# A mixture-of-experts kernel on Trainium2: TensorE's expert numbers loaded once for six tiles instead of once for each

## What is computed

```python
logits = xt @ Wr + br
probs = jax.nn.softmax(logits, axis=-1)
top_p, top_idx = jax.lax.top_k(probs, 2)
weights = top_p / top_p.sum(axis=-1, keepdims=True)
xn = (xt - mu) * jax.lax.rsqrt(var + LN_EPS)
xe = xn[None, :, :] * ln_g[:, None, :] + ln_b[:, None, :]
h = jax.nn.gelu(jnp.einsum('end,edh->enh', xe, W1) + b1[:, None, :], approximate=False)
y = jnp.einsum('enh,ehd->end', h, W2) + b2[:, None, :]
sel = jnp.take_along_axis(jnp.transpose(y, (1, 0, 2)), top_idx[:, :, None], axis=1)
out = (weights[:, :, None] * sel).sum(axis=1)
```

## Time and profile before

| | |
|---|---|
| median of 3 runs | 1020.41 us (1019.91 to 1022.8) |
| the profiled execution's own time | 1021.31 us |
| its span in the profile | 1019.3 us |
| PE busy | 752.5 us, 74% |
| PEld busy | 647.6 us, 64% |
| DVE busy | 611.3 us, 60% |
| ACT busy | 583.5 us, 57% |
| POOL busy | 483.2 us, 47% |

### The profile page before, as it was taken

How to read it: one execution, slowest core, us unless ns; L and a number is a source line. 1 busy time by engine, 2 the same in 40 slices (tenths; PEclk the granted TensorE clock), 3 DMA queues, 4 the chain that set the end, 5 groups by cost and what they waited for, 6 DMA issues and landing times. The chain is left out here.

```text
span 1019.3 us, 24538 instructions
## 1 busy us (share of the span) xinstructions
PE 752.5 (74%) x7306; PEld 647.6 (64%) x7307; DVE 611.3 (60%) x1820; ACT 583.5 (57%) x1157; POOL 483.2 (47%) x539
## 2 busy tenths in 40 slices
PE   2787795655579555542199999999959899899995
PEld 1665695444469544420178878888748788788784
DVE  6556402633752467977077877787736666666663
ACT  2667734655553435341176767767637677667763
POOL 4566400000275720577445656665545555555554
PEclk9989998567689879757599999999989999999998
DMA  7978413644311484412533333333323333333340
GB/s 222 235 231 258 116 32 106 183 125 143 115 56 37 156 251 142 139 56 75 182 98 114 111 119 113 118 117 109 111 85 90 112 106 113 114 116 110 110 123 29
DMA packets 127285, 126.87 MB, mean 124 GB/s; under 512 B 22471, under 2 KB 95454, under 8 KB 127106
## 3 DMA queue, kind: packets, MB, share of 16 engines
q1 hardware_dynamic: 92914, 82.73, 27.9%
q0 software_dynamic: 15296, 34.64, 9.6%
q10 hardware_dynamic: 19024, 8.86, 3.1%
HBM read 79.48 MB, written 49.09 MB: 126 GB/s over the span
## 5 line engine op out<-in xcount | busy, mean ns | idle before, releaser
L967 DVE TENSOR_TENSOR AB<-AB 128x512 f16<-128x512 f32 x280 | 192.3, 687 | 73.9 <-ACT AB L603 68.6
L397 POOL DMA_INDIRECT row_dram<-rows,idx x128 | 127.2, 994 | 203.3 <-DVE rows L775 165.3
L425 POOL DMA_INDIRECT row_dram<-B x140 | 144.0, 1029 | 111.8 <-DVE B L973 77.2
L425 POOL DMA_INDIRECT out<-B x140 | 140.1, 1001 | 116.4 <-DVE B L973 91.1
L600 ACT ACTIVATE AB<-ps 128x512 f16<-128x512 f32 x280 | 168.1, 600 | 41.3 <-PE ps L1155 40.4
L1172 PE MATMUL ps<-PPb,AB 128*128 x1120 | 185.3, 219 | 0.0
L1173 PE MATMUL ps<-PPb,AB 128*128 x1120 | 185.2, 219 | 0.0
L603 ACT ACTIVATE AB<-ps 128x512 f32<-128x512 f32 x280 | 169.1, 604 | 0.0
L1153 PE MATMUL ps<-B,PPb 128*128 128x256 f16 x560 | 154.7, 276 | 0.5 <-issue 0.5
L1154 PE MATMUL ps<-B,PPb 128*128 128x256 f16 x560 | 154.3, 276 | 0.0
L1155 PE MATMUL ps<-B,PPb 128*128 128x256 f16 x560 | 154.3, 275 | 0.0
(11 more groups left out here) (201 smaller groups left out, 1483.7 us busy)
## 6 DMA issues: line engine op xcount, KB each, us to landing
B<-row_dram SPq DMA_DIRECT2D x70, 264.0 KB
B<-row_dram SPq DMA_DIRECT2D x70, 136.0 KB
rows<-in_x SPq DMA_DIRECT2D x32, 256.0 KB, 5.0
rows<-in_L_conv_protein_pair SPq DMA_DIRECT2D x16, 512.0 KB, 4.3
g_dram<-work ACTq DMA_DIRECT2D x32, 256.0 KB, 3.1
work<-g_dram SPq DMA_DIRECT2D x32, 256.0 KB, 2.7
ABT<-in_x SPq DMA_DIRECT2D x32, 256.0 KB, 3.0
ABT<-in_L_conv_protein_pair SPq DMA_DIRECT2D x16, 512.0 KB, 4.0
```

What stands on the lines that cost most here:

```text
L397: pool.indirect_dma_start(row_dram, bass.IndirectOffsetOnAxis(ap=idx[:, j:j + 1], axis=0), rows[:, j, :], None).then_inc(scattered[b], 16)
L425: pool.indirect_dma_start(out_rows if second else row2_dram, bass.IndirectOffsetOnAxis(ap=Rw[:, u, b, at:at + 1].bitcast(u32), axis=0), Rw ...
L967: dve.tensor_tensor(Hp[:, hs, 1, :], Hf[:, q, :], Hp[:, hs, 0, :], ALU.subtract).then_inc(h_parts[q], 1)
```

## The change

The table `experts` becomes one number for each step, with zeros in front and behind. TensorE has seven registers, and one load fills all seven with the experts of seven tiles in a row, enough for six steps, as a step needs those of two neighbouring tiles. The load stands in the last of the six steps (`u == RING - 1`), between the first and the second half of the up products; `begin` copies the two that a step needs (`nc.snap`) at the step's head, and loads by itself only at the beginning of each list. The two waits at L1128 and L1148 are left out. `two_lists` passes the step's place in the ring to `before`, and a stage named in `always` also runs in steps whose tile lies outside the list.

```diff
--- before.py
+++ after.py
@@ -60,16 +60,16 @@
             extra()
 
 
-def two_lists(eng, stages, depth, before=None):
+def two_lists(eng, stages, depth, before=None, always=None):
 
     longest = max(lag for lag, _ in stages)
     for second, low, high in ((0, 0, CUT), (1, CUT, TILES)):
 
         def step(n, u):
             if before:
-                before(n)
+                before(n, u, low)
             for lag, stage in stages:
-                if not isinstance(n, int) or low <= n - lag < high:
+                if not isinstance(n, int) or low <= n - lag < high or stage is always and n + 1 < high + longest:
                     stage(n - lag, (u - lag) % RING, second)
 
         def single(n0, n1):
@@ -175,8 +175,8 @@
         first_row = work[0:1, 1024:1024 + TILES].bitcast(i32)
 
         EFRONT = 3
-        EROWS = TILES + EFRONT
-        experts = work[0:1, 1408:1408 + 2 * EROWS].bitcast(i32).rearrange("p (n v) -> p n v", v=2)
+        EROWS = TILES + EFRONT + RING
+        experts = work[0:1, 1408:1408 + EROWS].bitcast(i32)
 
         class Choice:
 
@@ -909,8 +909,7 @@
             step(dve.tensor_tensor(Q[:, 0:NQ], Q[:, 0:NQ], passed, ALU.add))
             step(dve.tensor_scalar(Q[:, 0:NQ], Q[:, 0:NQ], float(NE * CT), None, ALU.min))
             dve.sem_inc(s.Q_done, 1)
-            dve.memset(experts[:, 0:EFRONT, :], 0)
-            dve.memset(experts[:, TILES:, :], 0).then_inc(s.fill_done, 1)
+            dve.memset(experts, 0).then_inc(s.fill_done, 1)
             fs = [0]
 
             def fstep(i):
@@ -943,9 +942,9 @@
             assert fs[0] == FSTEPS, fs
             dve.wait_ge(s.tbl_psum, 1)
             dve.wait_ge(s.fill_done, 1)
-            for v, table in enumerate((first_row, experts[:, EFRONT:, 0], experts[:, EFRONT - 1:EFRONT - 1 + TILES, 1])):
+            for v, table in enumerate((first_row, experts[:, EFRONT:EFRONT + TILES])):
                 i = dve.tensor_copy(table.rearrange("p (l t) -> p l t", l=LISTS),
-                                    ps[6 + min(v, 1)][0:1, 0:LISTS * P].rearrange("p (l t) -> p l t", l=LISTS)[:, :, 0:CUT])
+                                    ps[6 + v][0:1, 0:LISTS * P].rearrange("p (l t) -> p l t", l=LISTS)[:, :, 0:CUT])
             i.then_inc(s.tbl_done, 1)
 
             def norm(n, u, second):
@@ -1124,28 +1123,27 @@
                     pe.wait_ge(r_loaded[u], (n // RING) * 16 + 16)
                 else:
                     pe.wait_ge(s.xn_done, n + 1)
-                if not isinstance(n, int) or n >= 2:
-                    pe.wait_ge(s.xT_lo, n - 1)
                 for b in range(HALVES):
                     i = pe.transpose(ps[u % 2][:, b * P:(b + 1) * P], Rw[:, u, b, ROW:ROW2], ident[:, :])
                 i.then_inc(s.xT_psum, 1)
 
+            PEQ = [mybir.EngineType.PE]
+            coming = [pe.alloc_register(f"expert{k}") for k in range(RING + 1)]
             chosen = []
 
             def load_experts(n):
-
-                _, chosen[:] = nc.values_load_multi_w_load_instructions(
-                    experts[:, bass.ds(n, 1), :].rearrange("p n v -> p (n v)"), [mybir.EngineType.PE],
-                    min_val=0, max_val=NE - 1,
-                    skip_runtime_bounds_check_because="each is an expert of the table, or the zero beside them")
+                pe.reg_load(coming, experts[:, bass.ds(n, RING + 1)])
+
+            def begin(n, u, low):
+                if isinstance(n, int) and n == low:
+                    load_experts(n - u)
+                chosen[:] = [nc.snap(r, PEQ, min_val=0, max_val=NE - 1) for r in coming[u:u + 2]]
 
             def up(n, u, q):
 
                 hs = 2 * (u % 2) + q
                 x_ = chosen[1]
                 pe.wait_ge(s.xT_lo, n + 1)
-                if not isinstance(n, int) or n >= 2:
-                    pe.wait_ge(h_full[q], n - 1)
                 for k in range(2):
                     c = (2 * q + k) * P
                     w = lambda r: W1h[:, bass.ds(x_, 1), r, c:c + P].rearrange("p a m -> p (a m)")
@@ -1176,8 +1174,12 @@
                         if k == HC - 1:
                             i.then_inc(y_psum[b], 1)
 
-            two_lists(pe, [(1, xT), (2, lambda n, u, second: up(n, u, 0)), (2, lambda n, u, second: up(n, u, 1)),
-                           (3, lambda n, u, second: down(n, u))], 2, before=load_experts)
+            def next_experts(n, u, second):
+                if u == RING - 1:
+                    load_experts(n + 1)
+
+            two_lists(pe, [(1, xT), (2, lambda n, u, second: up(n, u, 0)), (0, next_experts), (2, lambda n, u, second: up(n, u, 1)),
+                           (3, lambda n, u, second: down(n, u))], 2, before=begin, always=next_experts)
 
 
 def kernel(**inputs):
```

## The result

| | median, us | runs |
|---|---|---|
| before, run beside it | 1021.61 (1019.91 to 1026.94) | 4 |
| after | 1011.64 (1010.24 to 1015.59) | 4 |

The ratio is 0.990, with a 95% interval of 0.985 to 0.995: faster by 1.0%, where 2.7% was predicted (993, range 976 to 1009). The direction is right and the size is not. The profiled execution took 1011.25 us with a span of 1008.9, so its steps can be laid beside those of before (1021.3 and 1019.3).

A forecast was written before the change was run, and what follows sets the result against it. TensorE's instruction stream was taken to bound the second list, a three-step transfer loop also to limit the first. Gains of 20 and 7 us gave -27 from 1021.3: 994, or 993 as a median; range 976 to 1009.

The forecast's parts named there:

- What bounds before, and how long an ordinary step can be: Second list: bound by TensorE's instruction stream at 3.50 us a step; the array alone would allow 3.02.
- The waits: TensorE's three dropped waits, already satisfied when reached: 0.3 to 0.4 us of sequencer work in all; they "end nothing".
- The sequencer's lead: TensorE's sequencer would be 0.4 us ahead of the array where the new load stands, mid up products.
- The load of seven: New load once in six steps: 1.0 us, stalling the array 0.65 us per six steps.
- Rival A: The load of seven is dear, 1.9 us: second list 3.33 a step, first about 3.42, total 1005; chance 0.2.
- The branch: Loop branch every sixth step on TensorE: some 0.25 us of stall, the sequencer having regained only 0.3 after the load.
- transfer loop: Second list: mix, store, load, landing and products over four steps, 12.1 us or 3.03 a step, under the forecast 3.17.
- scatter: Second list: transfer loop near the step's 3.17 us, so scatter costs a little, making 3.20.
- For the first list the loop: Three-step loop of mix, store, load and norm, 9.94 to 10.30 us: 3.37 a step for 3.48, gaining 7 us.
- GpSimd's issue: First list's loop: second store's issue takes 1.34 us, 0.98 undisturbed; the 0.36 is part of the 10.30 us turn.
- rival C: Transfers bind both lists as stores land later: second list 3.35, gain 10, first gains 2, total 1008; chance 0.1.

The follow-up runs named there:

- waits_ring8: Kernel before with the three waits left out, two numbers still loaded each step, and a ring of eight slots: 988.88 us, 0.967 of before.
- before_ring8: Kernel before with a ring of eight slots instead of six, tiles moved to the scattered rows' memory: 1014.03 us, 0.990 of before.
- quads6: Kernel after, six slots, padded table, two loads of four numbers (fourth and sixth step) instead of one of seven: 1002.60 us, 0.978 of before.
- after_ring8: Kernel after with a ring of eight slots and one load of nine numbers per eight steps: 967.82 us, 0.947 of before.
- aligned6: Kernel after, six slots, table padded so each load of seven starts on a 16-byte boundary: 1008.64 us, 0.984 of before.
- load_ring8: Kernel before, waits kept, with a ring of eight slots and one load of nine numbers per eight steps: 972.19 us, 0.953 of before.

## Why the prediction was off

**What bounds before, and how long an ordinary step can be: right.** The second list was bound by TensorE's stream. In after its ordinary step is 2.99 us (3.02 was worked out), and the transposes follow within 0.05 us of the last down product.

**The waits: over-sized, and under-valued in kind.** They were costed at 0.3 to 0.4 us of the sequencer for all three. `waits_ring8` against `before_ring8` gives (3.457 - 3.258) = 0.20 us a step for three in the second list, 0.07 each. But the text said that they "end nothing" and let the load carry the sum. In this list, which the stream bound, they were 0.2 us of the step; with them gone alone it reached 3.32, the whole of what the change gives.

**The sequencer's lead: 0.4 was taken, 0.3 to 0.9 measured, with a mean of 0.6.** The rule weighed there, of the Trainium skill, Advanced Engine Details and Errata (Sequencer Loop), would have hidden the load fully. The measured stalls say that it isn't: 1.05 us for a load of 1.77 with a lead of 0.9, 0.97 for one of 1.11 with a lead of 0.3, each time the load less the lead and some 0.2 behind it.

**The load of seven: 1.0 was taken, 1.05 to 1.19 and 1.70 to 2.10 in turn measured,** a mean of about 1.5. Rival A's price of 1.9 was half right, for every other load. The larger lead offset part of it: stalls of 11.1 us in the second list, against 0.65 x 11 = 7 predicted. That term is off by 4 us. The Trainium skill, Runtime: NRT & Kernel Launch (Instruction fetch mechanics), has about 200 ns a register even in bulk; the page speaks of loads from device memory, these are from SBUF. The loads off the boundary come to 1.77/7 = 0.25 a number; those on it don't agree with a price per number, at 0.33 us for four and 0.85 for nine.

**The branch: 0.25 predicted, 0.21 measured** in the step shown (0.32 - 0.11).

**The step that failed is the transfer loop's place in the sum.** For the second list the prediction put the loop at 3.03 us a step and concluded that "Its transfer loop leaves that standing", adding 0.03 for scatter. Measured: 3.35. The time above 2.99 is 0.36 x 67 = 24 us, of which the stalls at the load are 11.1. The gaps before the transposes are 10.1, where eleven branches explain 2 to 3; transfers end the wait in eleven of these gaps (4.7 us by the waits of 790 to 980).

The loop's own size was nearly right. Averaged over fifty tiles of the second list of after, by the starts in the trace, the turn is 3.65 us from a mix to the second store's issue, 2.55 to the load's, 2.8 to the landing (where TensorE waited for it) and 3.36 to the mix four tiles on: 12.4 where 12.1 was worked out, 3.09 a step for 3.03. Of the 10 us missed in this list some 4 are the stalls above; the rest is the scatter, put at 0.03 a step. In `quads6` the same turn comes to 12.2, 3.06 a step, the products with what is left of stalls and branches to 3.05, and the step is 3.25: two limits that lie side by side cost some 0.2 us a step beyond either, an estimate from these sums. The reading that fits: after a late step the store lands late, the tile six on starts late, and the steps that could make up for it are held. And a late transfer costs twice, as the sequencer then reaches the load with a lead of 0.3 (920.6 above). `quads6` has 13 waits for a transfer from 790 to 980; the ring of eight, with two more steps in the turn, has none and comes to 3.08 with stalls of its own left (3.3 us).

For the first list the loop was named, but was let shrink: "it gives 3.31 to 3.43, middle 3.37". It held its 3.48 in every version with six slots, between 3.45 and 3.55, whatever the stream did. The sum took one turn of 10.30 us and let it shrink by 0.36 as GpSimd's issue would take 0.98 instead of 1.34. Averaged over 56 tiles the turn is 10.44 before (three steps of 3.48) and 10.46 after, and that issue 1.07 and 1.05: there was less than 0.1 to gain from it. From the load's issue to the norm the mean is 2.64 us before and 2.71 after, where a load that VectorE waits for takes 2.6, so this part had no slack; with eight slots it is 7.0 in `after_ring8`. The gaps did shrink there, and came back elsewhere: beyond the spacing of a gap-free stream, TensorE lost 28.9 us ahead of the transposes before and 10.5 after, but 12.7 more at the load and some 5 more at the bias products. That is what a limit outside the engine looks like.

**So rival C was the nearest** (second list 3.35, first nearly unmoved, 1008), and it had been given one chance in ten. That it names the very 3.35 is in part luck: its reason was stores that land later, and from the second store's issue to the load that waits for it the means are 2.48 us before and 2.49 after in the first list, 2.77 and 2.55 in the second; and 11 of the 24 us are stalls at the load. What spoke for it stood in the text: SyncE waited for a store before 62 of the first list's loads, and the second list's loop was 0.17 under the forecast step, by an estimate from one turn.

**What stays open.** The ring of eight changes more than the number of slots: the loop's body is eight steps, so there are fewer branches and loads, the loads start on the boundary, and the tiles lie in another buffer. `quads6` shows that cheap loads at six slots don't free the first list, and `before_ring8` that slots, buffer and rarer branch together give the kernel before only 1%; a ring of eight slots with a loop body of six steps wasn't tried, and neither was the turn of the store and load at six slots made shorter. How the 24 us of the second list divide between stall and transfers is read from the trace, not separated by a run of its own.

## What to carry to other kernels

When an engine's stream gets shorter, work out the turn of the buffers with the same care: the steps that the slots leave must exceed store, load and the stages between them, with room for the largest single stall and for scatter, or the saving is handed back, as it was here with six slots. Make the ring longer first and measure the stream's edits there: the two halves of this change read +0.4% and -1.3% at six slots, and -3.7% and -2.3% at eight. And look for waits that are always satisfied in a stream bound by its sequencer: leaving out three of them was the whole gain here, with six slots.

## What the runs showed of the hardware

- A register load of the sequencer isn't priced by the number of values. From a boundary of 16 bytes, four took 0.33 us (`quads6`), seven 1.08 (`aligned6`) and nine 0.85 (`load_ring8`), all medians; two took 0.55; seven from 8 bytes off it 1.70 to 2.10 (after). A reading that fits all is one access of about 0.3 us for each aligned four and one of about 0.26 for each value left over (seven are 1 + 3, nine are 2 + 1, seven off the boundary 7), an estimate from these rows and not tested for other counts.
- Three satisfied semaphore waits cost TensorE's sequencer 0.20 us a step (`before_ring8` against `waits_ring8`, second list; 0.17 in the first, 3.40 against 3.23).
- A load in mid-stream stalls the array by what it exceeds the sequencer's lead, here 0.3 to 0.9 us, and 0.16 more. The lead is not fixed: in the four turns of after whose transposes had waited for a transfer it was 0.3. Two short loads stalled the second list by a seventh of one long one (1.6 us against 11.1), and the first list by over a third (4.7 against 12.7).
